# Expert routing's top-k taken out of its own stage and spread over the groups of the recurrence, with the stages reordered

## The reference

```python
xn = _layernorm(x)
s = recurrence(xn)                      # gated linear recurrence over the tokens, 4 heads
g = silu(moe(xn))                       # experts, below
x = x + s * g
# moe:
capacity = max(1, int(Sz * 2.0 / 8) + 1)              # 257 of 1024 tokens
scores = softmax(xn @ router_w.T)                      # per token, over 8 experts
gate_vals, sel_idx = top_k(swapaxes(scores, 1, 2), capacity)   # per batch and expert
h = gelu(xn[b_idx, sel_idx] @ w1[e] + b1[e])
out = zeros_like(xn).at[b_idx, sel_idx].add((h @ w2[e] + b2[e]) * gate_vals)
```

## Time and profile before

| | |
|---|---|
| Median of 3 runs | 4757.16 us (4753.58 to 4759.05) |
| The profiled execution | 4756.55 us |
| Its span | 4755.0 us |
| PE / DVE / ACT / POOL busy | 88% / 58% / 42% / 35% of the span |
| Granted PE clock, mean | 0.972 |

### The profile page before, as it was taken

One profiled execution on the slowest core, in us unless ns is written; L12 is line 12 of the kernel. 1 busy time (PEld: TensorE's weight loads), 2 busy tenths in 40 slices (PEclk: granted clock), 3 DMA queues, 4 the chain that ended last, 5 costly groups with the idle time before them and its releaser, 6 DMA issues. The chain is left out here.

```text
span 4755.0 us, 79873 instructions
## 1 busy us (share of the span) xinstructions
PE 4184.6 (88%) x28828; PEld 3312.2 (70%) x28828; DVE 2750.1 (58%) x5151; ACT 1982.0 (42%) x3702; POOL 1685.4 (35%) x1323
## 2 busy tenths in 40 slices
PE   6702999999999999969999999999996899999995
PEld 6602989889898889945655565656564777777774
DVE  4475333443334344436766676666663588888886
ACT  2202444544444454424444444444443444444441
POOL 1101444443444444333333333333331223333333
PEclk9999999999999999989999999999997899999998
DMA  6631232332323222210000000000001434444433
GB/s 205 210 150 57 41 65 41 63 54 48 62 46 62 48 55 44 36 37 19 24 24 23 24 23 23 24 23 23 23 19 62 108 93 97 108 107 100 95 71 40
DMA packets 251713, 294.54 MB, mean 62 GB/s; under 512 B 21344, under 2 KB 226400, under 8 KB 247264
## 3 DMA queue, kind: packets, MB, share of 16 engines
q0 software_dynamic: 85760, 117.74, 14.7%
q1 hardware_dynamic: 140000, 138.26, 9.2%
q10 hardware_dynamic: 25600, 33.56, 2.1%
HBM read 155.15 MB, written 134.35 MB: 61 GB/s over the span
## 5 line engine op out<-in xcount | busy, mean ns | idle before, releaser
L586 DVE TENSOR_TENSOR e_hTl<-e_hf,e_hTh 128x512 fp32r<-128x512 f32 x512 | 355.3, 694 | 795.7 <-ACT e_hTh L528 794.2
L1051 POOL TENSOR_TENSOR a_mix<-a_tmp,a_h 128x512 f32<-128x512 f32 x320 | 394.1, 1252 | 814.8 <-DVE a_tmp L1110 654.2
L447 POOL DMA_INDIRECT acc_d<-e_y,e_sids x256 | 404.5, 1580 | 715.7 <-DVE e_y L602 670.9
L527 ACT ACTIVATE e_hf<-ps_heads,e_b 128x512 f32<-128x512 f32 x512 | 356.1, 696 | 693.8 <-PE ps_heads L674 679.0
L674 PE MATMUL ps<-e_w2h,e_hTh 128*128 128x256 f32 x2048 | 580.1, 283 | 0.0
L674 PE MATMUL ps<-e_w2h,e_hTl 128*128 128x256 f32 x2048 | 576.5, 281 | 0.0
L674 PE MATMUL ps<-e_w2l,e_hTh 128*128 128x256 f32 x2048 | 571.3, 279 | 0.0
L674 PE MATMUL ps_heads<-e_xTh,e_w1h 128*128 128x512 f32 x1024 | 419.8, 410 | 27.4 <-issue 23.5
L674 PE MATMUL ps_heads<-e_xTh,e_w1l 128*128 128x512 f32 x1024 | 407.8, 398 | 0.0
L674 PE MATMUL ps_heads<-e_xTl,e_w1h 128*128 128x512 f32 x1024 | 407.7, 398 | 0.0
L674 PEld LDWEIGHTS ps<-e_w2h,e_hTh 128*128 128x128 f32 x2048 | 385.0, 188 | 19.8
(11 more groups left out here) (295 smaller groups left out, 9444.1 us busy)
## 6 DMA issues: line engine op xcount, KB each, us to landing
r_x<-in_L_attn_hidden_states SPq DMA_DIRECT2D x32, 512.0 KB
xn_d<-r_xn ACTq DMA_DIRECT2D x32, 512.0 KB, 3.2
xnT_d<-r_xT ACTq DMA_DIRECT2D x32, 512.0 KB, 3.5
acc_d<-r_zeros POOLq DMA_DIRECT2D x16, 1024.0 KB, 21.1
e_w<-in_L_ffn_w SPq DMA_DIRECT2D x16, 1024.0 KB
s_d<-a_s SPq DMA_DIRECT2D x32, 512.0 KB, 2.9
f_a<-acc_d SPq DMA_DIRECT2D x32, 512.0 KB, 3.8
f_x<-s_d SPq DMA_DIRECT2D x32, 512.0 KB, 5.2
```

The lines of the kernel that those rows point to most:

```text
L447: pool.indirect_dma_start(acc_d, bass.IndirectOffsetOnAxis(ap=sids[:, GT * q + t:GT * q + t + 1], axis=0), ys[r][:, t, :], None, compute_o ...
L527: nc.scalar.activation(hf[m % 2][:], ps[2 + m % 2][:], ACT.Gelu, bias=b1s[:, m:m + 1])
L586: nc.vector.tensor_tensor(hT[q % 2][1][:, m, :], hf[m % 2][:], hT[q % 2][0][:, m, :].bitcast(F32), ALU.subtract).then_inc(h_sb, 1)
L1051: nc.gpsimd.tensor_tensor(mix[n][:, m, :].rearrange("p (c t) -> p c t", c=GT), tmp[i % 2][:].rearrange("p (c t) -> p c t", c=GT), h[q % 2] ...
```

## The change

In the diff the parts stand in the order `build`, `route_phase` (POOL, DVE), and then `recurrence_phase` with `sequence`, SP, POOL, DVE and PE. The stages run in the order routing, recurrence, experts, layer two. The scores (`score`, 128 x 1024) now belong to `build` and outlive routing, which ends with their copy. The 33 rounds move into the recurrence: round 0 stands in DVE's set-up, and rounds 1 to 32 stand one in each group, cut in three: MAX in slot 5, MAX_INDEX and the copy of the values in slot 6, MATCH_REPLACE and the copy of the places in slot 7. The offset, the left-over trip through memory, the transposes and the copies to `idxT` and `gateT` stand at the end of the recurrence. The zeros are written by 32 DMAs of 512 KB from POOL, one in each group's slot 7, from a tile of half the size that is cleared in front of POOL's other set-up.

```diff
             route_phase(nc, ctx, ps, a["L0_attn_hidden_states"], xn_d, xnT_d, a["L0_ffn_router_w"], ident, score)
+            recurrence_phase(nc, ctx, ps, ps_heads, xnT_d, s0_d, acc_d, left_d, ident, score, idxT, gateT, idxL, gateL, a)
             experts_phase(nc, ctx, ps, xn_d, acc_d, ...)
-        recurrence_phase(nc, ctx, ps, ps_heads, xnT_d, s0_d, ident, a)
...
-            pool.wait_ge(logit_sb, NG + 2)
-            for a in range(N // (P * 8)):
-                pool.dma_start(acc_v[a], zeros[:]).then_inc(acc_out, 16)
-            pool.wait_ge(acc_out, 16 * (N // (P * 8)))
...
-            with dve.Fori(0, ROUNDS) as k:
-                oo = Order(dve, top_o, base + 5 * k)
-                oo.did(nc.vector.max(v8[:], score[0][:]))
-                oo.hold(spare)
-                oo.did(nc.vector.max_index(i8[:], v8[:], score[0][:]))
-                oo.hold(spare)
-                oo.did(nc.vector.match_replace(score[0][:], v8[:], score[0][:], -1.0))
...
+                    if extra and s == CHUNK:
+                        extra(g, s)
                     if s < LATE or s == SLOTS - 1:
                         piece_at(s)
                         chunk_at(s)
                     else:
                         chunk_at(s)
                         piece_at(s)
+                        if extra and s < CHUNK:
+                            extra(g, s)
...
+            sp.wait_ge(topped, 1)
+            sp.dma_start(left_d[0:1, :].rearrange("o p -> p o"), idxf[:, CAP - 1:CAP]).then_inc(left_out, 16)
+            sp.dma_start(left_d[1:2, :].rearrange("o p -> p o"), vals[:, CAP - 1:CAP]).then_inc(left_out, 16)
+            sp.wait_ge(left_out, 32)
...
             store(NE - 1, QB - 1)
+            sp.wait_ge(left_in, 32)
...
+            nc.gpsimd.memset(zeros[:], 0.0).then_inc(zeroed, 1)
             for operand in (xo, w2, xot, dw2, low, x1t, dlow):
...
             def chunk(g, j, q, u, first):
+                if u == 0:
+                    pool.wait_ge(zeroed, 1)
+                    pool.sem_inc(spare, 1)
+                    pool.dma_start(acc_v[bass.ds(g, 1)].rearrange("o p n -> (o p) n"), zeros[:]).then_inc(acc_out, 16)
...
+            def largest(k):
+                dve.wait_ge(top_o, 5 * k)
+                dve.sem_inc(spare, 1)
+                nc.vector.max(v8[:], score[:]).then_inc(top_o, 1)
+            def places(k):
+                dve.wait_ge(top_o, 5 * k + 1)
+                dve.sem_inc(spare, 1)
+                nc.vector.max_index(i8[:], v8[:], score[:]).then_inc(top_o, 1)
+                nc.vector.tensor_copy(vals[:, bass.ds(8 * k, 8)], v8[:]).then_inc(top_o, 1)
+            def strike(k):
+                dve.wait_ge(top_o, 5 * k + 3)
+                dve.sem_inc(spare, 1)
+                nc.vector.match_replace(score[:], v8[:], score[:], -1.0).then_inc(top_o, 1)
+                nc.vector.tensor_copy(idxf[:, bass.ds(8 * k, 8)], i8[:]).then_inc(top_o, 1)
+            nc.vector.max(v8[:], score[:]).then_inc(top_o, 1)
+            places(0)
+            strike(0)
             dve.wait_ge(w_in, 16 * (LOADS + 1))
...
+            def rounds(g, s):
+                if s == 5:
+                    largest(g + 1)
+                if s == 6:
+                    places(g + 1)
+                if s == 7:
+                    strike(g + 1)
+                    if isinstance(g, int) and g == GROUPS - 1:
+                        dve.wait_ge(top_o, 5 * ROUNDS)
+                        nc.vector.tensor_scalar(idxf[:], idxf[:], rowf[:, 0:1], None, ALU.add).then_inc(topped, 1)
...
-            sequence(dve, ahead, begin, piece, level, chunk)
+            sequence(dve, ahead, begin, piece, level, chunk, rounds)
+            dve.wait_ge(idx_t, 1)
+            for u in range(2):
+                nc.vector.tensor_copy(idxT[:, :, u], ps[6][:, u * P:(u + 1) * P])
+                last = nc.vector.tensor_copy(gateT[:, :, u], ps[7][:, u * P:(u + 1) * P])
+            last.then_inc(idx_done, 1)
...
             sequence(pe, ahead, begin, piece, level, chunk)
+            pe.wait_ge(topped, 1)
+            emptied(pe, GROUPS - 1, GATES + 1)
+            for u in range(2):
+                nc.tensor.transpose(ps[6][:, u * P:(u + 1) * P], idxf[:, u * P:(u + 1) * P], ident[:])
+                done = nc.tensor.transpose(ps[7][:, u * P:(u + 1) * P], vals[:, u * P:(u + 1) * P], ident[:])
+            done.then_inc(idx_t, 1)
```

More of the change, by code:

```diff
@@ L83, in phase_semaphores, with route_phase @@
     return sem
-def route_phase(nc, ctx, ps, x, xn_d, xnT_d, acc_d, left_d, router_w, ident, idxT, gateT, idxL, gateL):
+def route_phase(nc, ctx, ps, x, xn_d, xnT_d, router_w, ident, score):
     with ExitStack() as mem:
@@ L102, in route_phase @@
         wr = sb("r_wr", [P, KD, NE])
-        zeros = sb("r_zeros", [P, 2048])
         logit = sb("r_logit", [P, N // P, NE])
@@ L106, in route_phase @@
         red = sb("r_red", [P, N // P])
[L107 to L115, removed]
         x_in = [sem(f"r_x_in{r}") for r in range(2)]
@@ L226, in _ @@
             for h in range(2):
[L227 removed]
+                o.did(nc.vector.tensor_copy(score[:, h * 512:(h + 1) * 512], ps[h][:]))
             o.wait()
[L229 to L253 removed]
         @block.scalar
@@ L312, in _ @@
             last.then_inc(score_t, 1)
-            pe.wait_ge(topped, 1)
-            for h in range(2):
-                nc.tensor.transpose(ps[2 + h][:, 0:P], idxf[:, h * P:(h + 1) * P], ident[:])
-                last = nc.tensor.transpose(ps[4 + h][:, 0:P], vals[:, h * P:(h + 1) * P], ident[:])
-            last.then_inc(idx_t, 1)
 def experts_phase(nc, ctx, ps, xn_d, acc_d, w1, b1, w2, b2, ident, idxT, gateT, idxL, gateL):
@@ L737, in _, with recurrence_phase @@
             experts(pe, one)
-def recurrence_phase(nc, ctx, ps, ps_heads, xnT_d, s0_d, ident, w):
+def recurrence_phase(nc, ctx, ps, ps_heads, xnT_d, s0_d, acc_d, left_d, ident, score, idxT, gateT, idxL, gateL, w):
     with ExitStack() as mem:
@@ L812, in recurrence_phase @@
         one_level = sb("a_level", [P, P])
+        v8 = sb("a_v8", [P, 8])
+        i8 = sb("a_i8", [P, 8], U32)
+        vals = sb("a_vals", [P, ROUNDS * 8])
+        idxf = sb("a_idxf", [P, ROUNDS * 8])
+        rowb = sb("a_rowb", [P, 1], I32)
+        rowf = sb("a_rowf", [P, 1])
+        leftf = sb("a_leftf", [B, NE])
+        zeros = sb("a_zeros", [P, N // GROUPS // P * D])
         w_in = sem("a_w_in")
@@ L850, in recurrence_phase @@
         s0_out = [sem(f"a_s0_out{r}") for r in range(2)]
+        zeroed = sem("a_zeroed")
+        acc_out = sem("a_acc_out")
+        top_o = sem("a_top_o")
+        topped = sem("a_topped")
+        idx_t = sem("a_idx_t")
+        left_out = sem("a_left_out")
+        left_in = sem("a_left_in")
+        idx_done = sem("a_idx_done")
         spare = sem("a_spare")
@@ L891, in bank, with sequence @@
             return ps[6 + n % 2]
-        def sequence(eng, ahead, begin, piece, level, chunk):
+        def sequence(eng, ahead, begin, piece, level, chunk, extra=None):
             def group(j, q, first, left):
@@ L1063, in _ @@
             sequence(pool, ahead, begin, piece, level, chunk)
+            pool.wait_ge(acc_out, 16 * GROUPS)
         @block.vector
@@ L2144, in build @@
         with ExitStack() as mem:
+            score = mem.enter_context(nc.sbuf_tensor("score", [P, T], F32))
             idxT = mem.enter_context(nc.sbuf_tensor("idxT", [P, P, 2], U32))
```

50 lines of the change are left out of this document (11 added, 39 removed).

## The result

The changed kernel takes **4613.69 us** (median of 4 runs, 4612.39 to 4619.89) against 4758.06 us for the kernel before (4753.58 to 4759.05): a ratio of 0.970, 95% interval 0.9686 to 0.9715. That is 3.0% faster, inside the range and 22.7 us above the forecast of 4591. The profiled execution has a span of 4612.0 us, 143.0 us less than before.

A forecast was written before the change was run, and what follows sets the result against it. PE bounds the recurrence, DVE alone the top-k stage. Span 4755.0 - 172.5 + 6.0 + 0 + 0 = 4588.5 us; with 1.55 us beyond the span 4590.1, and 0.6 us to the median, 4591 us; range 4581 to 4617.

The forecast's parts named there:

- Removed, -172.5: Between the score copy and the next stage: 174.34 us go, one barrier of 1.84 us returns, so -172.5 us.
- Set-up, +6.0: Ahead of PE's first recurrence product: zero tile clearing 0.95, two small operations 0.4, round 0 4.66 us; sum +6.0 us.
- the fill's 0.95: In the recurrence's set-up: POOL clears the new zero tile first, delaying the index tables for DVE's masks by 0.95 us.
- Per group, 0: In each recurrence group: a round's 4.66 us of DVE work fits three gaps ended by PE, costing 0.
- The sequencer's 0 to +16 us: Extra waits and register steps in the loop body: up to 0.5 us a group over 32 groups, taken as 0.
- Zeros, 0: POOL's one zeroing DMA a group falls in 7.12 us of idle time, on DMA engines 7% busy: 0.
- Tail, 0: At the recurrence's end: transposes and copies lie under the last store with 1 us to spare: 0, at most +1.
- The port: MAX and MAX_INDEX beside POOL's `a_mix` in every group, each reading one SBUF tile: no effect taken.
- The first rival: Rounds and POOL shut each other out in the recurrence: 1.5 us a group, 48 us, 4639 us; chance 1 in 10.
- no slow start is gained or lost: At the three later stages' starts: each began with PE idle for tens of microseconds and still does; no cost.
- another sequence: At the stage borders: same number of stages and barriers, so the other two borders cost what they did.
- the clock's spread: PE clock dips in the recurrence may fall otherwise: 1 us either way at two in three of 13 passes, ±8.

The follow-up runs named there:

- doubled passes: Kernel with 64 idle TensorE instructions at the recurrence's start, each of the three top-k passes over the scores done twice: 4590.13 us (one run).
- round 0 moved to group 0: Kernel with 64 idle TensorE instructions, first top-k round and its two one-column operations moved into group 0, zeros filled during POOL's wait for weights: 4591.75 us.
- loads held back: Changed kernel with the `a_h` loads delayed until TensorE's level-1 products of the group are done: 4612.36 us.
- zeroing out of the loop: Changed kernel with the 32 zeroing DMAs issued by the eight groups outside the recurrence's loop, four each: 4612.16 us.
- order alone: Kernel before with only the order of stages changed, all 33 rounds and the zeroing left in routing: 4786.95 us.
- 64 ahead: Changed kernel with 64 one-word semaphore instructions on TensorE's queue at the recurrence's start: 4589.51 us, ratio 0.9641 to the kernel before; repeated, 4592.05 us.
- 128 ahead: Changed kernel with 128 one-word semaphore instructions on TensorE's queue at the recurrence's start: 4587.58 us.

## Why the prediction was right, and where it missed

The direction and size came from the first term. *Removed, -172.5*: -172.84, the barrier 1.61 instead of 1.84 us. *Set-up, +6.0*: +5.38; the round took 4.24 us instead of 4.66, presumably because the register steps of the old loop aren't in it, and the two small operations 0.34 (276.16 to 276.50) instead of 0.4. With the fill's 0.95 that makes 5.53; 0.15 us less remain unexplained. The mask step of the earlier trace rows that stands beside `a_delta` is there again, 1.85 us long, now as `a_level`.

*Per group, 0*: shown three times over, in its mechanism and not only in its sum. The idle time left is 1.11, 2.23 and 1.93 us where I had 1.0, 2.3 and 1.6; the period is unchanged; and a doubled round is still free. The fourth group of a pass takes 47.86 instead of 47.49 us, but it is 47.51 with doubled passes and 47.50 with round 0 moved to group 0, so that isn't the rounds' price; its cause I did not look for. The sequencer's 0 to +16 us were 0. *Zeros, 0*: shown by taking them out of the loop. *Tail, 0*: DVE's last copy ends at 1881.41, the last store is issued at 1880.69, and the experts begin at 1885.41; from S's last addition to the next stage's first instruction it is 27.0 us, 26.63 before. I had given the tail at most +1.

*The port.* The first rival needed MAX or MAX_INDEX to wait for `a_mix`. MAX8 begins at 928.29, in the midst of an `a_mix` pair (927.68 to 929.99), and takes 1.22 us. Not so for the eight-value copy, which showed 0.53 us against 0.15, hidden. The passes read one tile of SBUF and the copy reads and writes SBUF alone, so both are as the rule says that I had weighed (the Trainium skill, SBUF — State Buffer, section Who interferes with whom).

**The step that failed** is in the sum: "no slow start is gained or lost" and "another sequence" of stages at no cost. I asked what moving a stage does to barriers, clocks and buffers, and not what it does to the place of its loops in the program. The sum has no term for it, and that place was worth +25.3 us at five jumps. That my range held it is luck: the sequencer's and the clock's spread happened to be as large. The sequencer's term was 0, and the clock is at most the 4.7 us that lie behind the second stops. The profile of before showed a trace of it that I didn't follow: five stops of 1.42 to 2.02 us with "issue" as their end. My first reading of the earlier trace rows hid them: "31 groups, which take 47.2 us each" is a mean, in which the last group's 31.2 us make up for the five of 48.8 to 51.8; the others take 47.2 to 47.8 us.

*The start, +3.81*: from the first product to the first `a_Sf` it was 76.19 us, before 72.38. The other kernels took from 72.86 (loads held back) over 73.84 (zeroing out of the loop) and 73.92 to 76.21 (order alone), and one kernel 73.92 and 76.07 in two executions. So most of it varies by itself, by 2.2 us in one and the same kernel; that none of it is the change is not shown. I had no term for it; it lies in the clock's share of the range. *Experts -1.45 and layer two -3.65* are as small, and unexplained.

## What to carry to other kernels

Work fits under a bound engine by the gap and not by the sum: read what ends each gap, put a piece that leaves time to spare in it, and a second piece is free too, until one edge is met. A change that moves code moves the loops behind it, and each jump back may cost one stop or two by where the loop begins; so look for stops that end with "issue" at each jump, before and after, and if they grew, a few dozen idle instructions ahead of the loop, in a place where the engine waits anyway, are the cheapest experiment and sometimes the cure. Count them for all loops behind that place: 64 helped here, 16 did harm in the next stage. The first products of a loop count as cover: what stands there must last until the next piece is in.

## What the runs showed of the hardware that I had not expected

- An otherwise idle pad of 64 instructions made the kernel 24 us faster, and one of 16 made it 21 us slower (one run), through two different loops.
- Where PE runs out of instructions after a jump can be counted: in four kernels the place agrees to the product with one count modulo 256 (stops after 19, 15, 11 and 28 products).
- A jump back costs PE 1.4 to 2.0 us in the recurrence at best, 1.85 to 2.66 us where a second stop follows; the second is up to 3.55 us. The branch's own record is longer, 3.3 to 4.6 us, since PE still works on products that it already has; not taken, it is 0.08 us. In the experts' stage single jumps cost up to 4.4 us, and 8.3 us in a bad place.
- From PE's restart to its second restart it is 3.05 to 3.33 us without other loads, and 3.87 to 4.42 us in the changed kernel, beside loads that reach 309 GB/s (896 to 897 us).
- A single stop can be followed by the lower clock or not, and its length doesn't tell: with 64 ahead the 16 products of `a_vw` take 3.72 us behind the third jump's stop of 1.72 us and 5.41 us behind the fifth's of 1.50 us. Behind the second jump the granted clock is 0.50 from 888 to 891 us there, and the products take 5.41 us; with 128 ahead it stays at 1.00, and they take 3.72 us. That is why jump groups come in steps of about 1.6 us (48.8, 50.5, 52.1) from one pass to the next.
